# Second routed layer of a four-block transformer: where high parts, gating portions and transposes stand on four engines, and products that nobody reads

## What is computed

```python
logits = _l2norm(flat, -1) @ _l2norm(sim_matrix, 0) - jax.nn.sigmoid(gates)
gated = jax.nn.relu(logits)
mask = (gated > 0)
inactive = jnp.sum(mask, axis=1) == 0
_, top_idx = jax.lax.top_k(logits, MIN_E)           # MIN_E = 2
mask = mask + inactive[:, None] * sum(one_hot(top_idx))
rw = softmax(where(mask > 0, gated, -inf))          # (b, t, e)
q = einsum('btc,ech,bte->bth', hidden, q_proj, rw)  # k and v alike
attn = softmax(causal(q @ k.T * scale))
ao = attn @ v
out = einsum('bth,ehc,bte->btc', ao, o_proj, rw)
```

## The kernel before

| step | TensorE, behind the step's products | ScalarE, behind the high part | VectorE, behind the low part of the step before |
|---|---|---|---|
| 2 | `front_x` | | |
| 4 | `front_logits` | `front_x` | |
| 6 | | | `front_gate` (waits for the logits) |
| 7 | | | `front_best` |
| 8 | | | `front_second` (8 small instructions) |
| 9 | | | `front_mask` |
| 10 | `out_T` | `front_exp` | |
| 11 | | | `front_weights` |
| 12 | | | `add` |
| 14 | `front_parts` | | |
| 15 | | `front_parts` | |

## Time and profile before

### The profile page before, as it was taken

The page is one execution under the profiler, slowest core; times in us unless marked ns, Lnnn a source line. Parts: engine busy times, 40 slices in busy tenths (PEclk is TensorE's granted clock), DMA queues, the critical chain, the costliest instruction groups (busy, mean ns, idle before and its releaser), DMA issues. The chain is left out here.

```text
span 1826.0 us, 25615 instructions
## 1 busy us (share of the span) xinstructions
PE 1502.6 (82%) x8105; PEld 1027.9 (56%) x8125; DVE 1257.8 (69%) x2784; ACT 886.6 (49%) x1622; POOL 201.7 (11%) x191
## 2 busy tenths in 40 slices
PE   6999988886999999889848999999999888665005
PEld 5777765554666666566536665666667455432005
DVE  3988965875677766566646666666665578677984
ACT  3666545773665555555513223322332267447742
POOL 2111012130000000211310000000000111011410
PEclk9999998997999999999969999999999999878557
DMA  4000003220000000332122234423443122000001
GB/s 164 1 1 0 1 1 97 68 53 1 1 1 1 0 0 1 99 102 57 29 93 116 112 120 162 162 107 124 162 162 133 56 60 53 19 0 0 0 0 46
DMA packets 32700, 108.01 MB, mean 59 GB/s; under 512 B 8845, under 2 KB 12301, under 8 KB 23502
## 3 DMA queue, kind: packets, MB, share of 16 engines
q1 hardware_dynamic: 32590, 106.64, 17.3%
HBM read 85.38 MB, written 2.36 MB: 48 GB/s over the span
## 5 line engine op out<-in xcount | busy, mean ns | idle before, releaser
L1012 DVE TENSOR_REDUCE mP_a<-psY_a 128x8 f32<-128x512 f32 x192 | 128.1, 688 | 101.1 <-PE psY_a L838 101.0
L756 ACT ACTIVATE probs_a<-psX_a 128x512 f32<-128x512 f32 x192 | 109.0, 595 | 125.1 <-PE psX_a L865 124.3
L1797 ACT ACTIVATE xsh_f<-xs_f 128x512 fp32r<-128x512 f32 x128 | 79.4, 630 | 166.9 <-DVE xs_f L2025 166.9
L2417 PE MATMUL ps_f<-wT_f,xq_f 128*128 128x128 f32 x192 | 26.0, 300 | 125.4 <-DVE xq_f L2438 125.3
L1555 DVE SCALAR_TENSOR_TENSOR g_f<-psU_f,cols_f1w,t_f 128x512 f32<-128x512 f32 (+1 forms) x104 | 78.0, 750 | 72.6 <-ACT t_f L1368 70.6
L1901 PE MATMUL psX_f<-xs_f,wo_f2w 128*128 128x512 f32 x256 | 121.3, 606 | 2.1 <-DVE xs_f L2025 1.5
L1368 ACT ACTIVATE t_f<-psU_f,cols_f1w 128x512 f32<-128x512 f32 (+1 forms) x104 | 71.2, 684 | 76.1 <-PE psU_f L1434 76.1
L1450 PE MATMUL psO_f<-h_f,w_f1w 128*128 128x512 f32 (+1 forms) x208 | 107.6, 599 | 0.0
L2029 DVE TENSOR_TENSOR xsl_f<-xs_f,xsh_f 128x512 fp32r<-128x512 f32 x128 | 87.9, 687 | 16.0 <-ACT xsh_f L1797 14.9
L838 PE MATMUL psY_a<-ks_a,xs_a 96*128 96x256 f32 x384 | 94.4, 347 | 4.1 <-DMA xs_a<-ql_a 2.5
L865 PE MATMUL psX_a<-xs_a,ks_a 128*128 128x256 f32 x384 | 86.1, 324 | 13.3 <-ACT xs_a L745 13.3
(11 more groups left out here) (441 smaller groups left out, 4006.6 us busy)
## 6 DMA issues: line engine op xcount, KB each, us to landing
wq_f2w<-f_routes SPq DMA_DIRECT2D x16, 1024.0 KB, 4.7
wk_f2w<-f_routes SPq DMA_DIRECT2D x16, 1024.0 KB, 4.7
wv_f2w<-f_routes SPq DMA_DIRECT2D x16, 1024.0 KB, 4.6
ring_f2w<-f_routes SPq DMA_DIRECT2D x16, 1024.0 KB, 4.6
xs_a<-qh_a SPq DMA_DIRECT2D x168, 64.0 KB, 2.0
xs_a<-ql_a SPq DMA_DIRECT2D x84, 64.0 KB, 2.0
xs_a<-probs_a SPq DMA_DIRECT2D x36, 64.0 KB, 2.0
x_sb<-in_x SPq DMA_DIRECT2D x1, 2048.0 KB, 8.4
```

The lines of the kernel that those rows point to most:

```text
L756: nc.scalar.activation(probs[:, b % 2, g, :, :], psX[g % 2][:].rearrange("p (e t) -> p e t", e=2), ACT.Exp, scale=float(dv) ** -0.5).then_ ...
L1012: nc.vector.tensor_reduce(mP[:, b % 2, h // 2, col:col + 8], psY[h % 2][:].rearrange("p (h k) -> p h k", h=8), axis=AX.X, op=ALU.max).then ...
L1797: nc.scalar.activation(xsh[:, e % RING, :], xs[:, e % RING, :], ACT.Copy).then_inc(s("x_high").sem, 1)
```

## The change

Six edits, all in `layer2_ffn`. On ScalarE `store_o(j - 1)` moves from the end of iteration j - 1 to behind the high part of step 1 of iteration j (and, for the last, behind the loop), and the exponential moves from step 10 to 12. On TensorE `out_T` moves from step 10 to 12 and `front_parts` from 14 to 15. On VectorE the gating starts at step 7 and its second portion is cut in two (`front_inactive`, `front_second`); the weights move from 11 to 13, the add from 12 to 14. `keep_busy(n)` issues n products of `sel` into `psX`, which nobody reads: 80 in the layer's front and 52 in iteration 0.

```diff
 scalar, main(j, q):
                     nc.scalar.activation(xsh[:, e % RING, :], xs[:, e % RING, :], ACT.Copy).then_inc(s("x_high").sem, 1)
+                    if e == 1 and not is_first(j, 2):
+                        store_o(j - 1)
                     if not is_last(j):
                         if e == 4:
                             front_x(j + 1, 1 - q)
-                        elif e == 10:
+                        elif e == 12:
                             front_exp(j + 1)
...
                 if has_second_next(j):
                     front_squares(j + 2)
-                if not is_first(j, 1):
-                    store_o(j)
...
             run_mains(act, main)
+            store_o(ITERS - 1)
             store_o(ITERS)
 tensor:
-                    if e == 10 and not is_first(j, 2):
+                    if e == 12 and not is_first(j, 2):
...
-                        elif e == 14:
+                        elif e == 15:
                             if not is_first(j, 2):
                                 pe.wait_ge(s("x_added").sem, s("x_added").at((j - 1) * TPI))
                             front_parts(j + 1)
...
                 if is_first(j, 1):
+                    keep_busy(8)
                     for stage in stages.values():
                         stage()
+                        keep_busy(6)
+                    keep_busy(14)
                 else:
                     mix_o(j, stages)
+            def keep_busy(n):
+                for _ in range(n):
+                    nc.tensor.matmul(psX[:], common["sel"][:, 0, :], common["sel"][:, 0:4, :], start=True, stop=True)
+            keep_busy(16)
             front_x(0)
+            keep_busy(4)
             front_logits(0, 0)
+            keep_busy(24)
             front_parts(0)
+            keep_busy(36)
             run_mains(pe, main)
 vector:
-            def front_second(steps):
+            def front_inactive(steps):
                 steps.done(nc.vector.tensor_reduce(top[:], gated[:], axis=AX.X, op=ALU.max))
                 steps.done(nc.vector.tensor_scalar(inact[:], top[:], 0.0, None, ALU.is_le))
                 steps.done(nc.vector.scalar_tensor_tensor(lg[:], oh[:], -1e30, lg[:], ALU.mult, ALU.add))
+
+            def front_second(steps):
                 first_max(nc, steps, lg[:], oh2[:], gs[:], tmp[:], desc[:])
...
-                    if e == 12 and not is_first(j, 2):
+                    if e == 14 and not is_first(j, 2):
                         add(j - 2)
                     if not is_last(j):
-                        if e == 6:
+                        if e == 7:
                             steps = gate_steps(j + 1)
                             front_gate(j + 1, steps)
-                        elif e == 7:
+                        elif e == 8:
                             front_best(steps)
-                        elif e == 8:
+                        elif e == 9:
+                            front_inactive(steps)
+                        elif e == 10:
                             front_second(steps)
-                        elif e == 9:
+                        elif e == 11:
                             front_mask(steps)
-                        elif e == 11:
+                        elif e == 13:
                             front_weights(j + 1, steps)
```

## The result

| | before | changed |
|---|---|---|
| median of 4 runs | 1824.44 us (1821.03 to 1826.36) | 1795.33 us (1792.53 to 1796.97) |
| profiled execution (span) | 1827.8 us (1826.0) | 1794.5 us (1792.7) |
| this layer, start of the first squares' product to start of the last `out_T` | 916.95 to 1438.78, 521.8 us | 906.93 to 1407.09, 500.2 us |

The ratio is 0.984, 95% interval 0.982 to 0.986: 29 us faster, where 26.9 were forecast (1798.5 us, range 1791 to 1810).

The account below looks back on a forecast made before the run. TensorE, busiest with 440 of 477 us, was taken to wait mainly for VectorE's low part. Terms summed to -26.9 us, taking the profiled 1827.8 to 1800.9; with the median 2.45 lower, 1798.5 us, range 1791 to 1810.

Parts of the forecast that it names:

- high parts ahead of the eviction: Iteration boundaries: ScalarE makes steps 0 and 1 before waiting for the mix, shrinking TensorE's gaps except at iteration 4; -8.7 us.
- clock behind the gaps: Starts of iterations 3, 5, 6, 7: shorter gaps keep the clock up, 1.65 us each; -6.6 us, bounds 0 and 8.3.
- smaller portions: Steps 5 to 15: later, smaller gating portions stop VectorE delaying low parts, 21.55 us in iteration 5; -14.4 us in all.
- gates' transposes behind step 15: Iterations 1 to 6: gates' eviction delays scores to 2.85 us after the step, +0.65 us each; +3.9 us.
- front's unread products: Layer's front: 80 products raise the clock, so step 0 runs at 2.4 GHz; -2.2 us, bounds +1 and -3.
- iteration 0's unread products: End of iteration 0: 52 products cost 4.1 us but remove the next slow start; +1.1 us, bounds +3.8 and -1.5.
- the reason given: Ahead of iteration 4: the gap stays because the loop branches back there and VectorE idles 2.48 us; no gain.
- The new wait behind step 15: Rival, iterations 1 to 6: TensorE's idleness there loses the clock, six falls of 1.65 us; 1808.5 us, chance 0.16.
- VectorE stays late: Rival, gating steps: half the waits return at small instructions or the add, 7 us less gain; 1805.5 us, chance 0.12.
- Closing gaps returns no clock: Rival, iteration boundaries: shorter gaps bring no clock back; 1805 us, chance 0.12.
- The better one: Rival: iteration 4's gap closes as well and iteration 0's products cost nothing; 1791.5 us, chance 0.07.

Follow-up runs that it names:

- b3: Kernel before with only the output's eviction moved behind the high part of step 1; median 1807.5 us, ratio 0.991, layer 505.9 us.
- e2: Changed kernel with the old step numbers of the gating, exponential, out_T, add and gates' transposes; median 1808.5 us, layer 505.2 us.
- e6: Changed kernel with the gates' transposes back behind step 14, the add staying at step 14; median 1793.8 us, layer 491.7 us.
- e4: Changed kernel without iteration 0's 52 unread products, keeping the front's 80; one run, 1799.9 us, layer 492.4 us.
- e5: Changed kernel without the front's 80 unread products, keeping iteration 0's 52; one run, 1795.5 us, layer 495.7 us.
- c2: Changed kernel run again without any edit, for a second trace; one run, 1791.8 us, layer 492.4 us.
- e7: Changed kernel with iterations 2 to 5 written out instead of the loop of two bodies; median 1793.9 us, layer 491.4 us.
- e1: Changed kernel with the output's eviction back at the iteration's end, ahead of the high parts; median 1811.0 us, layer 504.1 us.

## Why the forecast was right, step by step

| step | forecast | changed, trace against trace | alone |
|---|---|---|---|
| high parts ahead of the eviction | -8.7 | -8.8 | -8.2 (b3) |
| clock behind the gaps | -6.6 | -6.2 | -7.8 (b3) |
| smaller portions | -14.4 | -13.1 | with the next: -9.9 (e2 back) |
| gates' transposes behind step 15 | +3.9 | +2.8 | +3.0 (e6 back) |
| front's unread products | -2.2 | +4.4 | -1.9 (e4), 0 over nine traces |
| iteration 0's unread products | +1.1 | +1.0 | +0.9 (e5) |
| last mix's clock | 0 | -1.7 | in 7 of 14 traces, whatever the kernel |
| sum | -26.9 | -21.6 | |

The middle column is the difference of lengths in the two first traces: the gaps sum to 12.9 and 4.15; steps 0 to 5 of iterations 3 to 7 to 65.7 and 59.5; steps 5 to 15 of iterations 0 to 6 to 166.8 and 151.3, of which seven times 0.35 is the moved transposes. With c2 in place of the first changed trace, the front's term is -1.7 and the clock's -7.8, and the sum -29.3. The medians' 29 lies near it, but the sum moves by 7.7 us from one trace of the changed kernel to the other, so that the forecast came within 3.2 us of the median is in part luck; the terms of the portions and of the eviction are shown one by one.

- *The high parts.* Right, size and exception: nothing was gained ahead of iteration 4, and e7 shows the reason given to be the right one.
- *The clock.* Near in size, not in cause. "Idle spells up to 1.75 us left the clock alone; those of 2.0 and more mostly did not" reads a rule about length out of one trace, and that trace has a row against it: behind the 0.78 and 1.54 us ahead of the last mix the clock fell there as well. Gaps of at most 0.7 us never lost it, so closing them was safe, and b3 shows the return, 7.8 us with one edit. Of these, 1.6 are at iteration 4, where the gap stayed, so a closed gap is not what returned it there. And gaps of 2.0 us kept it in e1 and gaps of 2.83 to 3.10 us kept it in six of nine traces. The rule of the Trainium skill (TensorE: Matmul & The Clock Gate, HAM oscillation) that blames longer gaps than these fails on the same rows: in the kernel before the clock fell behind ten of twelve gaps of 1.93 to 3.11 us. Not tried, and open: whether it is the regular distance between the kernel before's gaps, 61.0 to 62.1 us from iteration 3 on (58.1 to 59.8 in e1), that brings each gap to the same moment of the clock's own course. Open too is why e1's median is 15.6 us up when its layer is 11.7 us longer than c2's.
- *The portions.* Mis-sized by 1.3 us: steps 5 to 15 took 21.83, not 21.55. Steps 5, 13 and 14 took 0.10, 0.27 and 0.11 us more than 2.10 (and step 12 its 0.35), where I had 0.2 at one of them.
- *The gates.* The mechanism as forecast (scores 2.79 us after step 15, 2.85 forecast), the price 0.5 us an iteration and not 0.65, since the mix and the stages behind it take up some of the delay. I did not ask whether the move was needed: e6 shows it wasn't.
- *The front's products.* The step that failed. It took the read's landing as it was in the trace of before, and the clock's rise as fixed. With the products the landing is 1.5 us later in the mean, which eats the 2 us that the clock gives back, and products issued in order stand ahead of real work or run out too soon. The bound I gave, +1, was too narrow: +4.4 occurred twice in nine.
- *The rivals.* The new wait behind step 15 (1.55 us idle by the forecast, 0.83 and 0.23 in iteration 5) never lost the clock. "VectorE stays late" is refuted by the waits' list: its six waits, 7.6 us, all stand ahead of the first product of an iteration. "Closing gaps returns no clock" is refuted by b3. The better one, iteration 4's gap, needed e7's edit.

## What to carry to other kernels

When an engine serves both the next iteration's first operand and the last one's output, ask which of the two is read first, and put the wait for the other behind it: this one move of three lines was worth 16 of 29 us when it was made first (b3), and 10.7 when it was taken back last (e1), because the clock falls that went with it in b3 are not in e1's trace, but for one. Filler work belongs only where its engine waits for something later than the filler's own end; count the gap and issue that many, not between stages that others wait for. Several traces of the same stretch, with and without, tell more about it than one: here the first trace of a part said +4.4 us, a cleaner one -1.9, and fourteen together 0. Read small gains from stretches whose start and end are in the same code, because the launch as a whole moves by more.

## What the runs showed of the hardware that was not expected

- The clock falls in the same code in one launch and not in the next: four times between 785 and 855 us in the kernel before (0.91 granted), never in the changed one (1.00). Ahead of the last mix it fell behind the same two waits, 0.78 and 1.54 us, in seven of fourteen traces. With that and other causes that were not followed up, the start of this layer moves by 13.5 us between traces of identical code.
- At the loop's backward branch VectorE idles 2.5 to 2.8 us, in every trace but the two without the loop, where it does not idle at all; TensorE's gap there falls from 2.83 or more to 0.29. The row names the last semaphore's owner instead.
- The same 1024 KB read landed 4.2 to 4.6 us after its issue in the traces without unread products ahead of it, and 4.8 to 7.4 us in those with them.
